# Gated cross-attention and latent feed-forward on one core: buffers, clears, load order and a new written-out order of work

## The reference

```
x : [4, 256, 256]    ctx : [4, 256, 64]
xn = layernorm(x, eps 1e-5)
# 16 heads, K 128, latent widths 192 (query) and 64 (key and value)
q_r    = ((xn @ Wq.T) per head @ w_kc_q) @ W_qr          # [b, h, s, 64]
kv     = ctx * cos + rotate_half(ctx) * sin              # rotary
k_r    = kv @ W_kr per head                              # [b, h, l, 64]
attn   = softmax(q_r @ k_r.T)                            # over 256 keys
out    = ((attn @ kv) per head @ w_kc_kv.T) @ Wo.T
x      = x + tanh(g_xattn) * out
y      = layernorm(x, eps 1e-5)
thought = layernorm(y)[:, last] @ agg_w + agg_b
4 times: thought += gelu(layernorm(thought) @ d1_w + d1_b) @ d2_w + d2_b
f      = y + sigmoid(y @ gate_w + gate_b) * (thought @ bc_w + bc_b)
x      = x + tanh(g_ffn) * layernorm(f)                  # result [4, 256, 256]
```

## Time and profile before

| | us |
|---|---|
| three runs | 218.21, 220.31, 220.58 |
| median | 220.31 |
| the profiled execution, its own time | 219.66 |
| its span, first to last instruction | 217.9 |
| PE, DVE, ACT, POOL busy | 200.5, 171.1, 104.0, 77.4 |
| mean granted PE clock | 0.981 |

### The profile page before, as it was taken

One profiled execution on the slowest core, in us unless ns is written; L12 is line 12 of the kernel. 1 busy time (PEld: TensorE's weight loads), 2 busy tenths in 40 slices (PEclk: granted clock), 3 DMA queues, 4 the chain that ended last, 5 costly groups with the idle time before them and its releaser, 6 DMA issues.

```text
span 217.9 us, 6292 instructions
## 1 busy us (share of the span) xinstructions
PE 200.5 (92%) x2533; PEld 175.0 (80%) x2533; DVE 171.1 (79%) x407; ACT 104.0 (48%) x191; POOL 77.4 (36%) x161
## 2 busy tenths in 40 slices
PE   7699999889999998989999999999999999998950
PEld 5477988768789997878889878898987898897930
DVE  4166489989977799999697699686955798899785
ACT  2375676447458264336516565546544443615120
POOL 8960020023998529897300110000400204334072
PEclk9999999999999999999999999999999799999995
DMA  6999980719005846000000520001204000000001
GB/s 155 249 280 314 288 247 2 194 39 257 5 5 132 232 118 131 0 3 3 3 3 0 130 70 3 0 3 40 67 0 99 3 11 17 27 26 27 20 28 48
DMA packets 21716, 17.87 MB, mean 82 GB/s; under 512 B 5524, under 2 KB 19892, under 8 KB 21688
## 3 DMA queue, kind: packets, MB, share of 16 engines
q1 hardware_dynamic: 21688, 17.47, 31.4%
HBM read 12.16 MB, written 1.05 MB: 61 GB/s over the span
## 4 chain that ended last, share of the span: by engine, by line
PE 56%; DVE 25%; POOL 6%; issue 5%; DMA 3%; ACT 3%; POOLq 0%; SPq 0%; DVEq 0%; ACTq 0%
PE ps L1344 6%; PE ps L1331 5%; PE ps L1312 5%; PE ps L1333 5%; DVE row_max L1032 5%; PE ps L1180 4%; PE ps L1182 4%; PE ps L1181 4%; DVE q_split L1026 3%; DMA x<-in_x 3%; DVE q_split L1024 3%; PE ps L1393 3%; PE ps L1354 3%; PE ps L1436 2%; PE ps L1425 2%
## 5 line engine op out<-in xcount | busy, mean ns | idle before, releaser
L911 ACT ACTIVATE probs<-ps 128x512 f32<-128x512 f32 x64 | 36.5, 595 | 32.9 <-PE ps L1333 32.4
L817 POOL TENSOR_SCALAR var_eps<-mean_var 128x1 f32<-128x1 f32 (+1 forms) x29 | 7.3, 252 | 119.2 <-DVE mean_var L949 118.9
L1032 DVE TENSOR_REDUCE row_max<-ps 128x2 f32<-128x512 f32 x64 | 42.5, 681 | 2.7 <-PE ps L1312 2.3
L1344 PE MATMUL ps<-kv,probs 128*64 128x65 f32 x1024 | 34.9, 227 | 0.0
L1344 PEld LDWEIGHTS ps<-kv,probs 128*64 128x64 f32 x1024 | 32.4, 140 | 2.5 <-issue 1.7
L1331 PE MATMUL ps<-q_hi,kv_lo 128*128 128x512 f32 x64 | 27.7, 433 | 0.0
L1312 PE MATMUL ps<-kv_hi,q_split 128*128 128x256 f32 x128 | 26.0, 299 | 1.4 <-DVE q_split L1026 0.7
L1333 PE MATMUL ps<-q_split,kv_hi 128*128 128x512 f32 x64 | 25.5, 399 | 0.0
L1312 PEld LDWEIGHTS ps<-kv_hi,q_split 128*128 128x128 f32 x128 | 20.0, 189 | 4.3 <-issue 1.3
L1180 PE MATMUL ps<-xT_lo,A_hi 128*128 128x256 f32 x64 | 18.8, 293 | 0.9 <-DVE q_split L1026 0.7
L1180 PE MATMUL ps<-B_lo,ctxT_hi 128*128 128x256 f32 x64 | 18.6, 291 | 0.1
(11 more groups left out here) (151 smaller groups left out, 436.8 us busy)
## 6 DMA issues: line engine op xcount, KB each, us to landing
q_hi<-q_split SPq DMA_DIRECT2D x16, 256.0 KB, 4.4
wq<-in_L_xattn_Wq SPq DMA_DIRECT2D x4, 512.0 KB, 8.6
wo<-in_L_xattn_Wo SPq DMA_DIRECT2D x2, 1024.0 KB, 10.9
w_rest<-in_L_ffn_d_w SPq DMA_DIRECT2D x2, 1024.0 KB, 5.7
wkcq<-in_L_xattn_w_kc_q SPq DMA_DIRECT2D x8, 192.0 KB, 4.6
...
```

The costliest lines, as they stand in the source:

```text
L911: act.activation(probs[:, n % PROBS_BUFS, lb, :], bank(e), ACT.Exp).then_inc(free[place[e]], 1)
L1032: dve.reduce_max(row_max[:, s % 2, 2 * j:2 * j + 2], bank(e).rearrange("p (h l) -> p h l", h=2), AX.X).then_inc(free[place[e]], 1)
L1344: ins = pe.matmul(bank(e)[q:q + 64, hh * (DC + 1):(hh + 1) * (DC + 1)], probs[:, n % PROBS_BUFS, lb, hh * P + q:hh * P + q + 64], kv1[:, k ...
```

## The change

1. PROBS_BUFS is 6. 2. KEEP is 5. 3. The clear of q_hi's upper rows is the third (and last) of DVE's opening memsets, no longer POOL's, and POOL does not wait for it. 4. kv_rope works on two batches at a time: two rounds of four instructions in place of four rounds, with the cos and sin tables broadcast over the pair; kvT waits for one round. 5. agg_w and bc_w share one tile; bc_w is loaded at SP's step down 1, once agg has been used. 6. bc_rows takes its four row picks from a broadcast column of the identity; row_pick shrinks from 10 KB to 2 KB. 7. All five orders are new.

```diff
-PROBS_BUFS = 5
+PROBS_BUFS = 6
...
-KEEP = 12
+KEEP = 5
...
-                    sp.dma_start(bc_w[:, :, :], t["L0_ffn_bc_w"].rearrange("(b p) n -> p b n", p=P)
-                                 ).then_inc(bc_w_in, 16)
...
+                if e == ("down", 1):
+
+                    filled(sp, ("agg", 0))
+                    sp.dma_start(agg_bc_w[:, :, :], t["L0_ffn_bc_w"].rearrange("(b p) n -> p b n", p=P)
+                                 ).then_inc(bc_w_in, 16)
...
-            pool.memset(q_hi[64:P, :, :].bitcast(F32), 0.0).then_inc(q_hi_cleared, 1)
-            pool.wait_ge(q_hi_cleared, 1)
...
-                    for b in range(NB):
-                        kv = kv1[:, b, :, 0:DC]
-                        pool.tensor_tensor(kv, ctxt[:, b], rope_cos, ALU.mult)
...
-                        pool.wait_ge(kv_made, b + 1)
+                    for i in range(2):
+                        bs = slice(i * NB // 2, (i + 1) * NB // 2)
+                        kv, raw = kv1[:, bs, :, 0:DC], ctxt[:, bs]
+                        cos, sin = [r.unsqueeze(1).to_broadcast([P, NB // 2, LB, DC]) for r in (rope_cos, rope_sin)]
+                        pool.tensor_tensor(kv, raw, cos, ALU.mult)
...
+                        pool.wait_ge(kv_made, i + 1)
...
+            dve.memset(q_hi[64:P, :, :].bitcast(F32), 0.0).then_inc(q_hi_cleared, 1)
...
-                    pe.wait_ge(kv_made, 2 * e[1] + 2)
+                    pe.wait_ge(kv_made, e[1] + 1)
...
-                        ins = pe.matmul(bank(e)[:, i * D:(i + 1) * D], row_pick[:, 2 * e[1] + i, :], bc4[:, :],
-                                        start=True, stop=True)
+                        b = 2 * e[1] + i
+                        pick = row_pick[:, :] if b == NB else ident[0:NB, b:b + 1].to_broadcast([NB, P])
+                        ins = pe.matmul(bank(e)[:, i * D:(i + 1) * D], pick, bc4[:, :], start=True, stop=True)
```

More of the change, by code:

```diff
@@ new lines @@
+        "gate": (202, 241, 270, 372, 385, 394, 410, 420),
+        "w_parts": (6, 35, 38, 66, 68, 74, 85, 110, 116, 142, 186, 199, 214, 218, 268, 334),
+        "c_stats": (33, 243, 293, 306, 406),
+        "c_norm": (96, 258, 305, 356, 402),
+        "thoughtT": (176, 188, 226, 260, 288, 313),
+        "agg": (179,),
+        "up": (198, 229, 267, 290),
+        "down": (210, 242, 275, 298),
+        "downT": (216, 247, 278, 302),
+        "bc": (316,),
+        "bc_rows": (332, 333, 338),
+        "f_y": (235, 246, 345, 376, 388, 391, 399, 416),
@@ new lines @@
+        "gate": (211, 248, 277, 370, 379, 391, 411, 415),
+        "w_parts": (5, 38, 54, 59, 100, 117, 124, 129, 141, 152, 183, 200, 245, 270, 273, 285),
+        "c_stats": (162, 182, 222, 253, 286),
+        "c_norm": (167, 188, 226, 257, 289),
+        "thoughtT": (174, 202, 229, 265, 293, 320),
+        "agg": (181,),
+        "up": (207, 235, 274, 296),
+        "down": (214, 246, 278, 300),
+        "downT": (219, 252, 284, 304),
+        "bc": (324,),
+        "bc_rows": (244, 280, 389),
@@ new lines @@
+        "gate": (230, 248, 307, 378, 383, 401, 412, 421),
+        "w_parts": (18, 20, 71, 78, 93, 123, 130, 151, 156, 160, 182, 224, 231, 239, 299, 330),
+        "c_stats": (46, 109, 179, 310, 364),
+        "c_norm": (12, 155, 259, 291, 387),
+        "thoughtT": (72, 218, 295, 297, 315, 386),
+        "agg": (360,),
+        "up": (205, 233, 255, 282),
+        "down": (129, 173, 281, 359),
+        "downT": (103, 159, 273, 343),
+        "bc": (409,),
+        "bc_rows": (321, 327, 328),
+        "f_y": (208, 235, 266, 338, 348, 396, 410, 413),
@@ new lines @@
+        "gate": (46, 160, 185, 198, 339, 368, 400, 411),
+        "w_parts": (67, 77, 83, 84, 96, 109, 113, 118, 150, 156, 169, 203, 222, 225, 235, 241),
+        "c_stats": (138, 190, 254, 258, 299),
+        "c_norm": (163, 202, 280, 288, 388),
+        "thoughtT": (159, 206, 253, 309, 315, 337),
+        "agg": (293,),
+        "up": (183, 228, 252, 394),
+        "down": (99, 189, 267, 319),
+        "downT": (10, 224, 236, 386),
+        "bc": (414,),
+        "bc_rows": (358, 378, 383),
+        "f_y": (259, 325, 354, 376, 381, 398, 405, 419),
@@ new lines @@
+        "gate": (243, 262, 271, 295, 349, 403, 412, 420),
+        "w_parts": (18, 48, 58, 73, 86, 92, 133, 148, 150, 151, 155, 198, 257, 291, 354, 360),
+        "c_stats": (129, 147, 175, 230, 398),
+        "c_norm": (179, 194, 201, 330, 382),
+        "thoughtT": (82, 206, 260, 292, 297, 300),
+        "agg": (11,),
+        "up": (141, 165, 258, 308),
+        "down": (159, 283, 317, 376),
+        "downT": (192, 236, 248, 332),
+        "bc": (241,),
+        "bc_rows": (102, 240, 310),
+        "f_y": (256, 275, 314, 315, 374, 393, 411, 417),
@@ L1410, in _ @@
                     taken(pe, ("thoughtT", 0 if name == "agg" else STEPS + 1))
-                    w = agg_w if name == "agg" else bc_w
                     pe.wait_ge(agg_w_in if name == "agg" else bc_w_in, 16)
                     for kb in range(KB):
-                        ins = pe.matmul(bank(e)[0:WIDE, 0:D], thoughtT[:, kb, :], w[:, kb, :], start=(kb == 0),
+                        ins = pe.matmul(bank(e)[0:WIDE, 0:D], thoughtT[:, kb, :], agg_bc_w[:, kb, :], start=(kb == 0),
                                         stop=(kb == KB - 1))
```

540 lines of the change are left out of this document (239 added, 301 removed), and 60 rows, old and new, of the table SLOTS.

## The result

| | before | after |
|---|---|---|
| median of 14 runs each, us | 218.91 | 216.99 |
| lowest and highest, us | 218.1 to 220.58 | 215.99 to 218.78 |
| ratio (95% interval) | | 0.9898 (0.9872 to 0.9924) |
| span of the trace, us | 217.9 | 214.2 |

The changed kernel is 1.0% faster, 1.9 us. The traces differ by 3.7 us, more than the medians: the trace shown has one of the lowest spans of its kernel (two of 14 runs, at 215.99 and 216.03 us, have 214.2), and a stretch at half clock is in the trace of before and not in it. The runs of either kernel lie mostly in two groups some 1 us apart (before near 218.3 and 219.4, after near 216.2 and 217.3), so one trace says little of a total, and I compare traces stretch by stretch.

A forecast was written before the change was run, and what follows sets the result against it. TensorE was taken to set most of the time, with VectorE-bound stretches at 31 to 62 and 75 to 98 us. Terms sum to -2.9 from 219.66, so 216.8; half of 0.65 on top gives 217.1 us, range 214.9 to 220.8.

The forecast's parts named there:

- Head: 0 to 16 us: keys 0.7 us earlier, lost waiting for the fifth key-projection weights; 0 (bounds -0.7 and +0.8).
- qk_2 ahead: After the head: qk_2 ahead of two query folds delays VectorE's work on them; +0.2 us (0 to +0.6).
- x early: First VectorE-bound stretch: earlier load of x's other half removes VectorE's idle time near 45 us; -0.6 us.
- maximum up: First VectorE-bound stretch: row maximum that TensorE waits for at 58.27 goes two items up; -0.4 us (0 to -0.5).
- Up to the first up-projection: Second VectorE-bound stretch: same VectorE items plus one normalisation up to the update; 0 us (-0.1 to +0.4).
- from there to down_0: Between up- and down-projection: VectorE has 0.75 us less work, TensorE's 0.3 us wait disappears; -0.5 us (0 to -0.6).
- ctxT_7_1's wait: Ahead of the last ctx transposes: TensorE's wait shrinks; -0.15 us.
- rival 3: Shorter TensorE work at six producer-consumer hand-offs, 3.8 us in all, becomes waits behind VectorE's queue: 220.6 us; chance 0.15.
- Tail: After 205 us: VectorE's new order and five fillers bring the last transposes earlier; -1.15 us (-0.6 to -1.3; +0.5).
- Rival 1: 168.5 to 171.9 us: splitting ten matmuls from 64 small ones holds the clock, saving 1.6 us: 215.2; chance 0.2.
- Rival 2: Gains ahead of the tail are covered by later TensorE waits; only the tail's 1.15 us stays: 218.5; chance 0.23.
- My own sign of being wrong: TensorE's idle sum between 16 and 205 us as large as before: head and both stretches' terms failed.

The follow-up runs named there:

- e7: Changed kernel with the clear of q's upper rows on GpSimd, behind the keys and first two statistics: 220.43 us, ratio 1.0031 to the kernel before.
- e10: Changed kernel with the loads of the identity and first rotary weights exchanged, as the kernel before has them: 216.49 us, ratio 0.9888 to the kernel before.
- e5: Changed kernel again, unaltered: 217.17 us, ratio 0.9903 to the kernel before.
- e8: Changed kernel with the load of x's other half put back behind q's first transfers: 217.24 us, ratio 0.9913 to the kernel before.
- e2: Kernel before with the load of x's other half moved ahead of q's first transfers: 218.84 us, ratio 0.9989 to the kernel before.
- e9: Changed kernel with moves in ScalarE's, TensorE's and VectorE's orders meant to remove four new waits: 216.28 us, ratio 0.9884 to the kernel before.
- e12: Changed kernel with only e9's Gelu move on ScalarE and its moves of tile 3's and tile 2's normalisations on VectorE: 216.75 us, ratio 0.985 to the kernel before.
- e6: Changed kernel with tile 3's output normalisation behind tile 6's statistics and half of tile 2's last normalisation earlier on VectorE: 217.96 us, ratio 0.9937 to the kernel before.
- e4: Changed kernel with twelve fillers in place of five: 218.48 us, ratio 0.997 to the kernel before.

## Why the prediction was right, and where it wasn't

The total is right, 217.1 against 216.99, and the gain, 1.0%, is at the edge of what the runs tell. Step by step:

- **Head, 0.** Right in mechanism: the fifth pair of weights lands at 15.2 to 15.5 us in the traces with the old first loads and at 15.2 to 16.1 with the new ones, and x's transposes follow it (15.83 to 16.14, and 15.98 to 16.71, e7 apart). The keys' 0.7 are lost ahead of it, one part already behind the clear, which I had ended 0.65 us too early. The spread upwards is inside my bound of +0.8, but not by the reason that I gave for the bound: clear and keys did not exclude each other. The order of the first loads may make it (e10).
- **qk_2 ahead, +0.2.** +0.05 to +0.09 in six of ten traces, within its bounds; +0.37 to +0.77 in three others (e5's lie in TensorE's "issue" time near 22 us) is unexplained.
- **x early -0.6, maximum up -0.4.** The sum is right (-1.01), the parts are not: e8 gives x 0.5 of it, e2 in the old order 0.1 to 0.3, since one execution's wait was taken for the usual one.
- **Second stretch, -0.3.** Right to 0.04 in every trace. **agg_0's wait, 0:** the wait did shrink, and nothing came of it, right.
- **Up to the first up-projection 0, from there to down_0 -0.5.** Together wrong: +0.06. In the first part I took 0 out of "0 (-0.1 to +0.4)" and the upper bound came: the up-projection starts 11.20 us behind the aggregation and not 10.82 (0.36 to 0.38 later in all ten traces). Its wait for VectorE's update of x grew from 0.78 to 1.05 us, and the one normalisation more that VectorE does ahead of that update takes 0.40. (It is no point of equal work: one product of maxima, smax_4_0, has moved ahead of it, into that wait.) In the second part -0.32 came, 6.03 us in place of 6.35. The step that failed there is "the bound 0 for ScalarE, where a copy that waits for TensorE now stands ahead of the Gelu": I had named the reason and taken the other end. e9's move of the Gelu, with its table load of 1.28 us, gave a further 0.38.
- **98 to 165, 0.** Near: -0.18 and +0.29. In the first stands a new wait of 0.7 us ahead of thoughtT_3, for the bank of a query fold. Moving it (e9) cost more.
- **ctxT_7_1's wait, -0.15.** Wrong: +0.46. VectorE idles 0.52 us for GpSimd's reciprocal root inside the full stretch (f_norm_3), and each such idle time arrives at the last context. e9's and e12's 0.36 show it, and e7 by chance: there this wait was of 0.19 us, another of 0.26 for ScalarE was gone, and the stretch came out at -0.03. e6 shows that the place for that work is ahead of the wait for the output projection and not behind. This is rival 3's mechanism, at a place that I hadn't listed, at a sixth of its price; of the six hand-offs that I had listed none became the wait.
- **Tail, -1.15.** -1.32 (-1.47 and +0.15). The seven fillers are the whole term (e4). That VectorE's order is needed for it too is argued from rows: before, y was ready at 207.78, and five fillers from 205.62 would have ended at 207.1, so some 0.7 us of the gain would have been lost; no run has five fillers with the old order. The +0.15 at the end is in large part the last gate's product, 0.95 us in place of 0.85.
- **Rival 1, the clock, 0.2.** In the trace shown the stretch at half clock near 168 us is gone, 1.6 us; five of the other nine have one at another place. In the runs the rival is not borne out: both kernels have the two groups of clocks, and at like clocks the gain is the same or larger (e5).
- **Rival 2, tail alone, 218.5.** Beside the tail and the clock the stretches from 16 us on sum to -0.63 where I had -1.75 (0.08 - 1.01 - 0.33 + 0.06 - 0.18 + 0.29 + 0.46). So two thirds of the gain ahead of the tail did not arrive: half of what is missing is up to down_0 (0.56), half was given back at the last context transposes (0.61). My own sign of being wrong, TensorE's idle time between 16 us and the tail as large as before, is half there: 5.0 us in place of 5.9.
- **The total** fits by luck. I took 2.9 us off 220.0 (the execution's 219.66 and 0.3), and 220.0 is 1.1 above the median of the 14 runs of before; the gain that came is 1.9, so 1.0 short. The two errors cancel.
